# First attention layer of a four-layer graph network: 32-word edge records, and the edge-attribute products of two pairs in 64 rows each

## The reference, cut to what matters

```
qkv = h @ Wqkv + bqkv                              # q, k: 16 heads x 8;  v: 16 heads x 16
qe = q[s] * 8 ** -0.5 + (edge_attr_18 @ Wq_rpe + bq_rpe)
ke = k[t]             + (edge_attr_18 @ Wk_rpe + bk_rpe)
compat = einsum('ehd,ehd->eh', qe, ke)             # one number per edge and head
attn = segment_softmax(compat, s)
out = segment_sum(v[t] * attn, s)
```

## Time and profile before

| what | value |
|---|---|
| median of 3 runs | 9492.82 us |
| lowest and highest | 9490.55, 9502.11 us |
| span of the profiled execution, first to last instruction | 8061.1 us |
| the median less that span | 1431.7 us |
| mean granted TensorE clock over the span | 0.850 |
| busy share PE / DVE / ACT / POOL | 72% / 60% / 46% / 64% |

### The profile page before, as it was taken

One profiled execution on the slowest core, in us unless ns is written; L12 is line 12 of the kernel. 1 busy time (PEld: TensorE's weight loads), 2 busy tenths in 40 slices (PEclk: granted clock), 3 DMA queues, 4 the chain that ended last, 5 costly groups with the idle time before them and its releaser, 6 DMA issues. The chain is left out here.

```text
span 8061.1 us, 137570 instructions
## 1 busy us (share of the span) xinstructions
PE 5841.1 (72%) x30934; PEld 4392.7 (54%) x30935; DVE 4854.8 (60%) x15153; ACT 3694.4 (46%) x10958; POOL 5168.4 (64%) x5180
## 2 busy tenths in 40 slices
PE   4777766656569989986988888699555555677774
PEld 3666655555546666653666666566334444455553
DVE  6766656666657777776988888621222223455555
ACT  0333323222347666663877777534000001777773
POOL 2777776777767666752766666410677773777773
PEclk8877777777789999997999999899777777777887
DMA  5222232111145555544666666511444443444443
GB/s 181 57 56 52 55 87 47 34 34 34 34 105 146 139 140 137 138 112 141 194 178 173 181 181 179 147 62 63 110 108 108 108 108 74 109 109 109 109 109 85
DMA packets 1038816, 872.85 MB, mean 108 GB/s; under 512 B 746697, under 2 KB 855265, under 8 KB 1038215
## 3 DMA queue, kind: packets, MB, share of 16 engines
q0 software_dynamic: 259600, 655.15, 29.6%
q1 hardware_dynamic: 723795, 158.04, 10.0%
q10 hardware_dynamic: 54948, 54.63, 2.0%
HBM read 733.27 MB, written 134.17 MB: 108 GB/s over the span
## 5 line engine op out<-in xcount | busy, mean ns | idle before, releaser
L1146 POOL DMA_INDIRECT edges_kv<-kv,edges_rec x1712 | 1826.5, 1067 | 841.9 <-issue 456.2
L1256 PE MATMUL banks<-edges_kv,edges_hot 128*128 128x288 f32 (+2 forms) x5136 | 1503.2, 442 | 325.8 <-DVE edges_kv L1531 272.0
L1256 PEld LDWEIGHTS banks<-edges_kv,edges_hot 128*128 128x128 f32 x5136 | 1039.5, 211 | 640.2 <-issue 319.7
L1712 POOL DMA_INDIRECT edges_rows<-rel,edges_rec x856 | 809.5, 946 | 382.3 <-issue 256.5
L498 POOL DMA_INDIRECT by_src_records<-sort_by_src_rec,sort_pos_i x808 | 795.1, 984 | 371.4 <-issue 232.6
L1146 POOL DMA_INDIRECT edges_kv<-feat,edges_rec x856 | 834.0, 974 | 269.0 <-issue 240.6
L1728 PE MATMUL banks<-edges_rows,edges_hot 128*128 128x256 f32 x1712 | 626.3, 530 | 466.4 <-DMA edges_rows<-rel,edges_rec 460.7
L498 POOL DMA_INDIRECT by_dst_records<-sort_by_dst_rec,sort_pos_i x808 | 787.0, 974 | 269.3 <-issue 237.5
L582 DVE SCALAR_TENSOR_TENSOR sort_junk<-banks,sort_hot_lo 128x128 bf16<-128x128 f32 x1616 | 439.0, 288 | 646.1 <-PE banks L638 634.7
L1728 PEld LDWEIGHTS banks<-edges_rows,edges_hot 128*128 128x128 f32 x1712 | 430.9, 264 | 662.2 <-DMA edges_rows<-rel,edges_rec 310.3
L1373 ACT ACTIVATE edges_off<-columns,edges_column 128x128 bf16<-128x128 f32 x2568 | 784.6, 390 | 0.0
(11 more groups left out here) (434 smaller groups left out, 12052.6 us busy)
## 6 DMA issues: line engine op xcount, KB each, us to landing
edges_kv<-kv,edges_rec POOLq DMA_INDIRECT x1712
sort_feat<-in_edge_attr_dram SPq DMA_DIRECT2D x100, 256.0 KB
rel<-tables_stage SPq DMA_DIRECT2D x100, 252.0 KB
by_dst_records<-by_dst_blank ACTq DMA_DIRECT2D x1, 17120.0 KB, 56.9
edges_rec<-by_dst_records SPq DMA_DIRECT2D x26, 640.0 KB
edges_rows<-rel,edges_rec POOLq DMA_INDIRECT x856
edges_kv<-feat,edges_rec POOLq DMA_INDIRECT x856
by_src_records<-sort_by_src_rec,sort_pos_i POOLq DMA_INDIRECT x808
```

The source lines that it names most:

```text
L1146: pool.indirect_dma_start(kv[:, r, c, 0:koff + DIM], None, tab, bass.IndirectOffsetOnAxis(ap=reci[:, b, c, idx:idx + 1], axis=0)).then_inc ...
L1256: last = pe.matmul(ps[:, 6 + m % 2, 0:OW], hot[:, b % 2, c, :], kv[:, b % BUFS, c, koff:koff + OW], start=(c % 2 == 0), stop=(kind != 1 an ...
L1712: pool.indirect_dma_start(rows[:, r, c, :], None, tab, bass.IndirectOffsetOnAxis(ap=reci[:, b, c, idx:idx + 1], axis=0)).then_inc(gathered ...
```

## The change

Four edits. The `by_src` record becomes 32 words wide, so that 4 tiles make 128 partitions and each pair of tiles 64. `w_attr` shrinks to 64 rows for each pair (its third index is now the tile within the pair). The attribute product of an even pair takes partitions 0 to 63 and that of an odd pair partitions 64 to 127, each into its own bank, and both are issued one behind the other, ahead of the q products of both. And `body` is replaced by `body_by_halves` for this layer, where `expand` is called for two pairs at a time.

```diff
-            w_attr = ph.sbuf("w_attr", [K, G // 2, 2 * QW])
+            w_attr = ph.sbuf("w_attr", [K, 2, 2 * QW])
...
-                            sp.dma_start(w_attr[r0:r0 + O.attrs, c, cols], w).then_inc(weights_in, 16)
+                            sp.dma_start(w_attr[r0:r0 + O.attrs, c % 2, cols], w).then_inc(weights_in, 16)
...
+                    if kind == 0:
+                        if not (isinstance(j, int) and j == 0 and PAIRS * b + pairs[1] < 3):
+                            pe.wait_ge(edges_used, n(PAIRS, pairs[1]) - 2)
+                        pe.wait_ge(front_copied, n(1, 1))
+                        for m in pairs:
+                            mine = slice(K // 2 * (m % 2), K // 2 * (m % 2) + K // 2)
+                            pe.matmul(ps[:, BANKS[(PAIRS * b + m) % 3], :], attr_t[mine, b % 2, m // 2, :],
+                                      w_attr[mine].rearrange("k c w -> k (c w)"), start=True, stop=False, skip_group_check=True)
                     for m in pairs:
...
-                        if not (isinstance(j, int) and j == 0 and PAIRS * b + m < 3):
+                        if kind == 1 and not (isinstance(j, int) and j == 0 and PAIRS * b + m < 3):
                             pe.wait_ge(edges_used, n(PAIRS, m) - 2)
                         pe.wait_ge(hot_t_ready, n(2, m // 2 + 1))
-                        if kind == 0:
-                            pe.wait_ge(front_copied, n(1, 1))
-                            u = 2 * (m % 2)
-                            pe.matmul(ps[:, bank, :], attr_t[:, b % 2, m // 2, :], w_attr[:, u:u + 2, :].rearrange("k c w -> k (c w)"),
-                                      start=True, stop=False, skip_group_check=True)
...
+                def body_by_halves(j, b):
+                    inside = b < size(j)
+                    older, oldest = lagging(j, b, 1), lagging(j, b, 2)
+                    ahead, beyond = (after(j, b, 1), after(j, b, 2)) if inside else (None, None)
+                    if older:
+                        turn_scores(*older)
+                    if inside:
+                        expand(j, b, (2, 3))
+                    if oldest:
+                        sums(*oldest, 0)
+                    if ahead:
+                        spread_lo(*ahead, 1)
+                    if older:
+                        turn_back(*older)
+                    if ahead:
+                        expand(*ahead, (0, 1))
+                    if oldest:
+                        sums(*oldest, 1)
+                    if beyond:
+                        front(*beyond)
...
-        by_src = make_order(nc, ctx, "by_src", 18, 24, one=18, seg=19, lo=20, idx=21)
+        by_src = make_order(nc, ctx, "by_src", 18, 32, one=18, seg=19, lo=20, idx=21)
```

More of the change, by code:

```diff
@@ L1117, in _ @@
                             cols = slice(i * QW, i * QW + QW)
-                            sp.dma_start(w_attr[r0:r0 + O.attrs, c, cols], w).then_inc(weights_in, 16)
+                            sp.dma_start(w_attr[r0:r0 + O.attrs, c % 2, cols], w).then_inc(weights_in, 16)
                             r0 += O.words["one"]
-                            sp.dma_start(w_attr[r0:r0 + 1, c, cols], bias.rearrange("(o n) -> o n", o=1)).then_inc(weights_in, 16)
+                            sp.dma_start(w_attr[r0:r0 + 1, c % 2, cols], bias.rearrange("(o n) -> o n", o=1)).then_inc(weights_in, 16)
                 records = O.rec.rearrange("(t p) w -> p t w", p=P)
@@ L1326, in body_by_heads @@
                         sums(*oldest, 1)
+                if kind == 0:
+                    body = body_by_halves
                 if kind == 3:
```

## The result

| kernel | median | lowest to highest, runs | clock over the span |
|---|---|---|---|
| before | 9497.47 us | 9490.55 to 9502.91, 4 | 0.775 (a second profile, below) |
| changed | 9658.88 us | 9649.83 to 9672.28, 4 | 0.757 |

The ratio is **1.0172, 95% interval 1.0154 to 1.0190**: the change costs some 161 us. The forecast was 9700 us, slower with a chance of 0.87. The profiled execution of the changed kernel took 9662.19 us with a span of 9660.3.

What follows compares the result with a forecast made beforehand. TensorE, in a cycle with VectorE, was taken to bound the first attention layer's 12.12 us step. The new cycle through ScalarE adds 0.83 and the clock 1.1: 14.05 us, 107 x 1.93 = +207, 9700 us; range 9540 to 9790.

Steps and rivals of the forecast that it cites:

- The cycle: First attention layer: turn of the scores, products, sums and ScalarE's chain up to its attr_t copy close a one-step cycle, 12.95 us.
- The product term A: A half-step's two attribute products on TensorE: three passes, 1.29 us, plus 0.18 for row switches, 1.47; bounds 0.86 and 1.91.
- The register load: TensorE's load L969 behind the wait for the turn, no longer covered by the sums: 0.49 us per step, bounds 0 and 0.6.
- The chain term: Step of the first attention layer at full clock grows from 12.12 to 12.95 us, +0.83 per step, +89 us over 107.
- The clock term: TensorE's pauses lower its granted clock to a mean of 0.86, adding 1.1 us per step, bounds 0 and 2.0.
- Nearer to the even spread: Why 1.1 us was taken: half-clock time lying anywhere in the step costs 0.8 us, all on the cycle's TensorE part 2.0.
- The sum against the time: Profiled span 8061.1 us, median 1431.7 above it and taken as untouched by the change; 9492.8 + 207 = 9700 us.
- The signs: Expected in the layer: step 12.9 to 14.8 us, L1233 idle about 2 us, clock 0.8 to 0.9, b1 starting with a2.
- The clock holds: Rival, 27%: slower by ScalarE's chain in the first attention layer at unchanged clock, +43 to +136 us, likeliest +89, 9582 us.
- Faster: Rival, 6%: products fully side by side without switch price, load hidden, both together under 1.13 us; 11.85 us per step, 9464 us.
- 64-row products run one behind the other: Rival inside the slower cases, no chance of its own: nothing side by side, 1.91 us per half-step, 13.39 us step, +136 us.
- Edits taken at nothing: Wider by_src records in scatters, loads and blank fill, more partitions in the copy, smaller w_attr: no cost.

Runs made afterwards that it cites:

- e: Changed kernel with the register load of the blocks issued ahead of the wait for the turn of the scores; 9595.34 us, ratio 1.0081 to the kernel before.
- h: Changed kernel with ScalarE's two front copies ahead of its first L1371 instead of behind it; 9617.04 us, ratio 1.0112 to the kernel before.
- i: Changed kernel with early register load, two filling products ahead of the wait and sooner ScalarE front copies; 8033.94 us against 8066.46 before, ratio 0.9959.
- d: Changed kernel with the products of pairs 2 and 3 ahead of the turn of the scores; 9495.88 us, ratio 0.9979 to the kernel before.
- b: Kernel before with only the new TensorE order, 24-word records and 96-row products kept; 9644.47 us, ratio 1.0139 to the kernel before.
- g: Changed kernel with two products nobody reads (1.7 us) ahead of the wait for the turn of the scores; 9539.18 us, ratio 1.0025 to the kernel before.
- f: Kernel before with 32-word records alone, products of 128 rows, old order; 9513.58 us, ratio 0.9995 to the kernel before.
- c: Changed kernel with the old TensorE order, so 32-word records and 64-row products alone; 9518.53 us, ratio 1.0008 to the kernel before.

## Why the prediction was right, and where its sizes were off

- **The cycle.** Right. L1233 follows ScalarE's `attr_t` copy by 0.10 us in at least nine of ten steps, and comes 3.4 us behind the front's end in the mean, where TensorE has nothing else to do. In the ordinary execution of the kernel before, TensorE's idle time there was 1.4 us per step already, so "where before it was hardly ever so" holds for the short execution alone, and ScalarE's chain, "not yet binding", released the turn in at least half of the steps. What is taken out of either part shortens the step (e, h), and in i the parts add up to the step, 11.33 us. Exchanging two calls undoes the loss (d), and the order alone makes it (b).
- **The product term A**, forecast 1.47. At the full clock four passes start within 0.54 us and are done in 1.06, and the way into and out of 64 rows costs 0.09 and 0.10 (0.20 instead of 0.11 us from L1247 to L1209, 0.21 instead of 0.11 to the second q pass). That makes 1.25. The step "the order of issue allows three passes" was wrong: the passes start in twos, in most steps 7 ns apart. But a pass takes 0.52 instead of 0.43. The rule of the Trainium skill's page "TensorEngine Tiling (Array Packing)", that tiles run independently (section "Key Properties"), is borne out. The twofold of its section "Theoretical Speedup" holds here against two products of 64 rows one by one (2 x 1.05 us against 1.06), and not against the two of 96 rows that stood here. Measured, 1.25 us replace 1.72, a factor of 1.4.
- **The register load**, forecast 0.49: 0.60 - 0.11 = 0.49. Right in size. That hiding it would give 87 us, and not the 43 expected of e, was not foreseen.
- **The chain term**, +0.83 per step. Where executions are short, i gives an estimate of 12.66 - 12.00 = +0.66, in line with the smaller A. Where they are long, g and the kernel before have the same step (14.02 and 14.03) although g has the whole chain: +0.0. The likely reason is that the kernel before had lost as much there to its pauses, which no run tests.
- **The clock term**, +1.1 with bounds 0 and 2.0: measured 1.47 by g. Mechanism and bounds right, the choice too low. "Nearer to the even spread" was wrong: the falls come behind the pause, on the cycle. Slow stretches also reach TensorE's other half-step: ScalarE's L1388 waits 0.5 us in the mean for the front, with the filling 0.1.
- **The sum against the time.** This step failed. "What lies around the span, which the change doesn't touch" was an ordinary execution's own slowness, spread over all stages, this one too (14.03 us per step instead of 12.00). The forecast of +1.93 stands on a step of 12.12; against 14.03 the change gives +1.46. That the time came within 42 us is luck, due to two errors that go against each other, the chain term too high by 0.83 there and the clock too low by 0.37.
- **The signs.** Those on the mechanism came: L1233 waits, the load stands behind it (0.60 us to L1209), the clock is 0.83, the four passes take 1.06 us. Three did not come as written. The step is 15.49 us, outside the 12.9 to 14.8; TensorE's idle time ahead of L1233 is 3.3 us per step and not 2; and the product of one pair does not wait for the other's first pass.
- **The rivals.** "The clock holds" is what g makes by hand, and there the change would cost 0.25%; so in the long executions the clock is some 85% of the loss (1.47 of 1.72 in hundredths of the time). "Faster" fell with its condition: load and A together are 1.74, not under 1.13. "64-row products run one behind the other" is excluded by rows. Edits taken at nothing: f and c bear them out.

## What to carry to other kernels

In an order written by hand, look at what stands ahead of each wait: with 1.3 us of products ahead of it the wait left TensorE idle for 0.2 us per step (1.4 in the long executions), and the same wait uncovered put the products on a cycle through two engines and took the clock with it. An idle time of 3.3 us per step on TensorE cost 1.5 us more behind it, because what comes right behind it ran at half the clock; two products that nobody needs gave back 140 of 161 us. And compare a profile's span with the times of the runs before using it: here they differed by 1431.7 us where they should by 2, the profile was of another kind of execution, and its waits were not those of the median.

## What the hardware showed that was not expected

- fp32 products of 64 rows on different row halves start within 7 ns of each other and take 0.52 us per pass of 512 columns, alone as well as side by side (at the full clock); passes of 96 rows, and of 128 in the filling of g, take 0.43.
- Taking a register load of 0.3 us from behind a wait to ahead of it gave 0.53 us per step, part of it clock, and 1.7 us of needless work per step made the kernel 140 us faster.
- The same kernel takes 8066 us in one batch and 9497 to 9520 in others, and the batches whose chip is on record (8066; 9505; 9520) ran on three different ones. The single scatters and gathers are as long; between them there are pauses of some microseconds, on VectorE and ahead of the scatters above all, which the profile puts down to "remote" or "issue". What makes them was not found.
